# The last attention period of a fused adaLN, attention and two-stage expert kernel, re-ordered on one core

## What is computed

```python
xc  = modulated(x, cond) @ W          # scaled by cond, then demodulated
q, k, v = split(xc @ w_qkv.T); q, k = rope(q), rope(k)     # 16 heads of 8
p   = softmax(causal(q @ k.T / sqrt(8)))
x1  = x + (p @ v) @ w_out.T
s   = sigmoid([x1, cond] @ W_router.T); the two best of s + bias give the gates
x2  = (shared_experts(x1) + sum_e gelu(x1 @ r_w1[e].T) @ r_w2[e].T * gate_e) / 4
w   = softmax weights of the best 3 of 8 zones, from tanh(mean(x2) @ W1 + b1) @ W2 + b2
out = x1 + x2 + sum_z gelu(x2 @ Wa[z]) @ Wb[z] * w_z
```

## Time and profile before

| | us |
|---|---|
| median of 3 runs (lowest, highest) | 181.64 (181.29, 181.72) |
| the profiled execution | 180.98 |
| its span | 179.1 |
| PE busy | 168.9 |
| DVE busy | 138.9 |
| ACT busy | 134.3 |
| POOL busy | 93.8 |

### The profile page before, as it was taken

The page is one execution under the profiler, slowest core; times in us unless marked ns, Lnnn a source line. Parts: engine busy times, 40 slices in busy tenths (PEclk is TensorE's granted clock), DMA queues, the critical chain, the costliest instruction groups (busy, mean ns, idle before and its releaser), DMA issues.

```text
span 179.1 us, 3278 instructions
## 1 busy us (share of the span) xinstructions
PE 168.9 (94%) x943; PEld 116.8 (65%) x944; DVE 138.9 (78%) x444; ACT 134.3 (75%) x224; POOL 93.8 (52%) x117
## 2 busy tenths in 40 slices
PE   6899999899999999988999999996999989999992
PEld 2656575565666666653758767864687867788881
DVE  5588989989898899980586999699799658637551
ACT  3569177688768888889734787953879999999970
POOL 5508088985463969688532522021769931676000
PEclk9999999999999999999999999999999999999999
DMA  4824775676686567520110899960760000001001
GB/s 144 294 46 107 191 203 159 218 234 213 166 267 208 143 194 194 164 94 5 62 51 17 231 345 344 347 178 4 241 230 0 0 4 0 0 2 59 0 4 59
DMA packets 15349, 24.28 MB, mean 136 GB/s; under 512 B 2844, under 2 KB 4828, under 8 KB 15308
## 3 DMA queue, kind: packets, MB, share of 16 engines
q1 hardware_dynamic: 14532, 23.29, 42.2%
q10 hardware_dynamic: 800, 0.79, 1.7%
HBM read 18.71 MB, written 5.27 MB: 134 GB/s over the span
## 4 chain that ended last, share of the span: by engine, by line
PE 70%; DVE 11%; ACT 7%; issue 6%; POOL 4%; DVEq 0%; ACTq 0%; POOLq 0%
PE psum L1407 11%; PE psum L1540 10%; PE psum L1541 9%; PE psum L1542 9%; PE psum L1467 8%; PE psum L1443 7%; PE psum L1286 3%; PE psum L1338 2%; PE psum L1352 2%; ACT t_probs L1105 2%; DVE psum L772 2%; DVE t_raw L924 1%; PE psum L1402 1%; ACT t_q_pad L1155 1%; PE psum L1447 1%
## 5 line engine op out<-in xcount | busy, mean ns | idle before, releaser
L772 DVE CUSTOM_DVE_ANT_0 psum<-psum,t_causal 128x128 f32<-128x128 f32 (+3 forms) x128 | 58.6, 525 | 5.8 <-PE psum L1407 3.0
L1105 ACT ACTIVATE t_probs<-psum 128x1024 f32<-128x1024 f32 (+2 forms) x48 | 40.9, 883 | 8.2 <-PE psum L1443 5.2
L1407 PE MATMUL psum<-t_stacked,t_q_pad 96*128 96x256 f32 (+2 forms) x104 | 33.3, 391 | 0.5 <-DVE t_row_max L772 0.2
L1407 PEld LDWEIGHTS psum<-t_stacked,t_q_pad 96*128 96x128 f32 x104 | 18.4, 189 | 12.4 <-DVE t_row_max L772 10.2
L672 POOL TENSOR_SCALAR_AFFINE_SELECT t_probs<-t_probs 128x512 f32<-128x512 f32 x32 | 20.5, 651 | 9.0 <-ACT t_probs L1105 9.0
L944 DVE SCALAR_TENSOR_TENSOR t_q_pad<-psum,t_zw_all,t_q_pad 128x512 fp32r<-128x512 f32 x24 | 17.8, 748 | 9.3 <-ACT t_q_pad L1153 9.2
L1139 ACT ACTIVATE psum<-psum 128x512 f32<-128x512 f32 x40 | 23.4, 586 | 0.9 <-PE psum L1542 0.3
L703 POOL TENSOR_TENSOR t_q_pad<-t_raw,t_q_pad 128x512 fp32r<-128x512 f32 x8 | 10.8, 1357 | 21.0 <-ACT t_q_pad L1155 21.0
L1467 PE MATMUL psum<-t_probs,t_v_all 128*32 128x512 f32 (+3 forms) x256 | 20.6, 439 | 0.0
L772 DVE DVE_READ_ACCUMULATOR2_ANT t_row_max<- 128x1 f32 x128 | 18.0, 141 | 0.0
L1153 ACT ACTIVATE t_q_pad<-psum,t_zw_all 128x512 fp32r<-128x512 f32 x24 | 16.5, 688 | 1.2 <-PE psum L1542 0.6
(11 more groups left out here) (233 smaller groups left out, 369.6 us busy)
## 6 DMA issues: line engine op xcount, KB each, us to landing
t_stacked<-scratch SPq DMA_DIRECT2D x16, 256.0 KB, 5.7
t_probs<-in_L_ffn_Wa SPq DMA_DIRECT2D x2, 1024.0 KB, 11.5
scratch<-t_o_sb SPq DMA_DIRECT2D x7, 256.0 KB, 2.1
t_raw<-in_experts SPq DMA_DIRECT2D x7, 256.0 KB, 3.6
t_stacked<-scratch SPq DMA_DIRECT2D x9, 192.0 KB, 3.7
t_q_pad<-scratch SPq DMA_DIRECT2D x28, 48.0 KB
scratch<-t_dn_hi SPq DMA_DIRECT2D x2, 512.0 KB, 3.4
t_q_two<-scratch SPq DMA_DIRECT2D x5, 192.0 KB, 2.6
```

The lines of the kernel that those rows point to most:

```text
L772: last = V.tensor_tensor_reduce(scores, scores, causal[:, S - width:S], 1.0, 3 * BIG, ALU.add, ALU.max, row_max[s][:, qb, j:j + 1])
L1105: A.activation(o, scores, ACT.Exp, scale=float(1.0 / np.sqrt(np.float32(HD)))).then_inc(exp_done, 1)
L1407: last = T.matmul(bank[:, o:o + width], q_pad[s][0:TOP, j, qb * P:(qb + 1) * P], stacked[0:TOP, n, 0:width], start=True, stop=True)
```

## The change

Seven edits, all in the order of work; nothing of the arithmetic changes.

1. The laying of group 7's maxima goes to a ring bank (7) and not to a half of the exp slots. POOL places them after the first mask of period 6, not before the second. The copy of the laid rows goes from ACT to DVE, behind `residual(0)`.
2. `normalise(0)` on DVE goes from behind unit (7, 10) to behind (7, 7), `project_out(0)` on PE from period 7 to period 6.
3. In period 6 PE has scores 3, the projection, the laying, scores 4 and 5, and V product 0 last.
4. Period 7 is written out on PE: V products 1 to 3 of group 6 stand between the scores of group 7, the router behind them, then scores 2 to 5, `up(0)`, and all V products of group 7.
5. The router's logits lie in bank 7, their exp is taken behind exp 1 of group 7.
6. Splits and loads of the expert weights come half a period earlier.
7. `take_outputs(6)` on DVE goes behind the high and low parts of x1. `invert(1)` goes from ahead of the unit loop to i = 1, `normalise 1` from i = 3 to 4.

```diff
-RING_ORDER += [("out", 0), ("route", 0)]
+RING_ORDER += [("out", 0), ("lay", GROUPS - 1)]
+LAST = GROUPS - 1
 AT = {
-    "normalise 1": [3],
+    "invert 1": [1],
+    "normalise 1": [4],
...
-INV_AT = [(6, 8), (7, 10)]
-SPLITS = {(3, 0): 0, (3, 2): 1, (4, 0): 2, (4, 2): 3, (5, 0): 4, (5, 2): 5, (6, 0): 6}
-EXPERT_LOADS = [(), (0, 1), (2, 3), (4, 5), (6,), (), (), ()]
+INV_AT = [(6, 8), (7, 7)]
+SPLITS = {(2, 2): 0, (3, 0): 1, (3, 2): 2, (4, 0): 3, (4, 2): 4, (5, 0): 5, (5, 2): 6}
+EXPERT_LOADS = [(), (0, 1, 2), (3, 4), (5, 6), (), (), (), ()]
...
         def qm_bank(n):
-            return ST[:, slot_of("exp", n - 1, STU - 1) + 1, :] if n else ring("lay", 0)
+            return ST[:, slot_of("exp", n - 1, STU - 1) + 1, :] if 0 < n < LAST else ring("lay", n)
...
-                    if c == 1 and n + 1 < GROUPS:
+                    if c == 1 and n + 1 < LAST:
                         place_max(n + 1)
                     for o in ((0,) if c < 2 else (0, 2 * P)):
...
                     last.then_inc(masked, 1)
+                    if c == 0 and n + 1 == LAST:
+                        place_max(LAST)
...
+            def copy_last_qm():
+                dve.wait_ge(qm_full, GROUPS)
+                V.tensor_copy(q_mov[LAST % BUFS][TOP:ROWS, :], qm_bank(LAST)[TOP:ROWS, :]).then_inc(qm_copied, 1)
...
-            take_outputs(GROUPS - 2)
             residual(0)
+            copy_last_qm()
             x1_high(0)
             x1_low(0)
+            take_outputs(LAST - 1)
             dve.wait_ge(w_lo, len(range(0, UP_COLS, S)) + len(range(0, DN_COLS, S)))
             gates(0, 0) ... gates(0, 3)
-            invert(1)
             for i in range(N_UNITS + 1):
                 if i < N_UNITS:
                     finish_hidden(i)
                 if i:
                     hidden_lo(i - 1)
+                for _ in due("invert 1", i):
+                    invert(1)
...
-                bank = (ring("route", 0) if b == 0 else MISC)[:, 0:KB * EXPERTS]
+                bank = (MISC if b else QM)[:, 0:KB * EXPERTS]
...
                 exp(n, 1)
+                if n == LAST:
+                    exp_of_minus_logits(0)
...
-                if n + 1 < GROUPS:
+                if n + 1 < LAST:
                     copy_qm(n + 1)
-                if n == GROUPS - 1:
-                    exp_of_minus_logits(0)
...
-                    wait_ring("route", 0)
+                    pe.wait_ge(qm_copied, GROUPS)
...
-                    pe.wait_ge(expneg, 1)
+                    pe.wait_ge(mx_reduced, len(MX_LIST))
+                    pe.wait_ge(x1_ready, 1)
...
-            for n in range(GROUPS):
+            for n in range(LAST):
...
                 scores_for_exp(n, 2)
-                if n == GROUPS - 1:
+                scores_for_exp(n, 3)
+                if n + 1 == LAST:
                     project_out(0)
-                scores_for_exp(n, 3)
+                    lay_max_under_q(LAST)
...
                 scores_for_exp(n, 4)
-                if n == GROUPS - 1:
-                    route_experts(0)
+                if n + 1 == LAST:
+                    scores_for_exp(n, 5)
                 weigh_v(n, 0, 0, S)
...
+            scores_for_exp(LAST, 0)
+            weigh_v(LAST - 1, 1, P, S)
+            scores_for_exp(LAST, 1)
+            weigh_v(LAST - 1, 2, 2 * P, S)
+            weigh_v(LAST - 1, 3, 3 * P, S)
+            route_experts(0)
+            scores_for_exp(LAST, 2)
+            scores_for_exp(LAST, 3)
+            scores_for_exp(LAST, 4)
+            scores_for_exp(LAST, 5)
             up(0)
-            weigh_v(GROUPS - 1, 1, P, S)
-            weigh_v(GROUPS - 1, 2, 2 * P, S)
-            weigh_v(GROUPS - 1, 3, 3 * P, S)
+            weigh_v(LAST, 0, 0, S)
+            weigh_v(LAST, 1, P, S)
+            weigh_v(LAST, 2, 2 * P, S)
+            weigh_v(LAST, 3, 3 * P, S)
```

More of the change, by code:

```diff
@@ L1412, in lay_max_under_q @@
                 pe.wait_ge(m_ready, n + 1)
-                if n:
+                if 0 < n < LAST:
                     wait_slot("exp", n - 1, STU - 1)
                 else:
-                    wait_ring("lay", 0)
+                    wait_ring("lay", n)
                 if n == 0:
@@ L1528, in route_experts @@
                 if b == 0:
-                    wait_ring("route", 0)
-                bank = ring("route", 0) if b == 0 else MISC
+                    pe.wait_ge(qm_copied, GROUPS)
+                bank = MISC if b else QM
                 T.matmul(bank[:, 0:KB * EXPERTS], temb[:, b, :], small[:, W_RT:W_RB], start=True, stop=True)
@@ L1659, in _ @@
                 scores_for_exp(n, 4)
-                if n == GROUPS - 1:
-                    route_experts(0)
+                if n + 1 == LAST:
+                    scores_for_exp(n, 5)
                 weigh_v(n, 0, 0, S)
-                maximum(7)
-                if n + 1 < GROUPS:
+                if n + 1 < LAST:
+                    maximum(7)
                     lay_max_under_q(n + 1)
-                maximum(8)
-                scores_for_exp(n, 5)
-                maximum(9)
-                maximum(10)
+                    maximum(8)
+                    scores_for_exp(n, 5)
+                    maximum(9)
+                    maximum(10)
+            scores_for_exp(LAST, 0)
[8 more added lines that the diff above has]
+            scores_for_exp(LAST, 5)
             up(0)
-            weigh_v(GROUPS - 1, 1, P, S)
-            weigh_v(GROUPS - 1, 2, 2 * P, S)
-            weigh_v(GROUPS - 1, 3, 3 * P, S)
+            weigh_v(LAST, 0, 0, S)
+            weigh_v(LAST, 1, P, S)
+            weigh_v(LAST, 2, 2 * P, S)
+            weigh_v(LAST, 3, 3 * P, S)
             for i in range(1, N_UNITS + LAG):
```

## The result

The changed kernel takes **184.94 us** (median of 4 runs, 183.93 to 186.01); the kernel before, run beside it, 181.68 (181.29 to 181.75). The ratio is 1.0196, 95% interval [1.016, 1.0232]. The change costs 3.3 us where the forecast said 0.7, outside its range of 180.7 to 183.0. The profiled execution took 185.37, its span 183.6, 4.5 more than before.

A forecast was written before the change was run, and what follows sets the result against it. It took the PE-led chain of waits, and when DVE's residual(1) runs, as the bound. +1.0 for the late residual(1) less 0.25 slack gave +0.75, stated as +0.7: median 182.3 us, range 180.7 to 183.0.

The forecast's parts named there:

- (2): DVE, period 6: normalise(0) moved forward collides with POOL's spreading and delays unit (7, 8) by 1.45 us.
- (4): PE, group 7 in the new order: second up starts at 93.25 against 93.56, 0.3 us gained.
- (5): invert(1) 3.1 us later; DVE waits for gate rows until 104.2; residual(1) at 108.9 against 107.89, 1.0 us later.
- (1): Splits and expert loads half a period earlier on ACT and SP: cost 0, at most 0.8 us, once.
- its sign of being wrong: An exp of period 3 that waits for ACT's split would show the splits and loads mispriced.
- the far end given: Upper delay for unit (7, 8): 2.1 us, if normalise(0) waits behind POOL's low part also, 79.17.
- the row in the middle: Delay of 1.45 us for unit (7, 8), from the DVE cast's row: 0.53 us beside POOL's masks.
- (3): Period 6: laying in a ring bank, POOL's place after the first mask; laying at 81.5 instead of 81.97, 0.5 gained.
- laying at 81.5, so 0.5 gained: PE, period 6: the laying for group 7 comes at 81.5 instead of 81.97, counted as 0.5 us gained.
- PE's gain: The 0.3 us by which PE's second up was to start earlier, 93.25 against 93.56.
- (6): Behind residual(1): small waits of DVE and ACT for PE soak up 0.25 us, taken from 0 to 0.5.

The follow-up runs named there:

- e9: Changed kernel with the sixth split moved to period 6's first place, so POOL has no low part behind the last spread; 183.45 us, ratio 1.014.
- e15: Changed kernel with two warm-up matmuls ahead of scores (7, 4) and the inverse behind unit 0 instead of unit 1; 183.54 us, ratio 1.0095.
- e5: Changed kernel with the splits and expert loads of before; 186.0 us, ratio 1.0213.
- e4: Kernel before with normalise(0) alone moved forward behind unit (7, 7); 182.26 us, ratio 1.0056.
- e6: e3 with normalise 1 at i = 3 and the splits and loads of before; 182.0 us, ratio 1.0037.
- e8: Kernel before with only invert(1) moved to i = 1 and normalise 1 to i = 4; 184.7 us, ratio 1.0142.
- e10: Kernel before with invert(1) moved behind finish_hidden(0), normalise(1) left at 3; 181.02 us, ratio 0.9984.
- e14: Changed kernel with two warm-up matmuls ahead of scores (7, 4) and nothing else; 185.13 us, ratio 1.0201.
- e1: Changed kernel with normalise(0) back behind unit (7, 10); 183.78 us, ratio 1.0129.
- e3: Changed kernel with normalise(0) back behind (7, 10), invert(1) at i = 0 and PE's projection behind the laying; 182.71 us, ratio 1.0051.
- e11: e6 with scores (6, 4) and V product (6, 0) ahead of the laying again; 182.1 us, ratio 1.0071.
- e2: Changed kernel with invert(1) alone moved up to i = 0, behind finish_hidden(0); 184.28 us, ratio 1.0179.
- e7: e3 with five warm-up matmuls in PE's wait for the maxima at 80 us; 182.49 us, ratio 1.007.
- e12: e6 with two warm-up matmuls in PE's wait at 90 us, ahead of scores (7, 4); 181.42 us, ratio 0.9999.

## Why the prediction was wrong

The forecast was +0.7 us, measured was +3.3. Four steps failed: the delay by `normalise(0)` in (2), 1.45 forecast and 2.64 measured; the stretch on PE in (4), 10.7 and 11.4; DVE's wait for the gate rows in (5), 1.8 and 3.0 to 3.3; and TensorE's clock, which stood in no term. Where the collision has the forecast's price (e9), the change costs 1.6 at full clock.

**(1) Splits and loads** at 0: its sign of being wrong, an exp that waits for ACT's split, is in the profile of e15 (ACT waits 1.97), and PE waits 0.2 to 1.2 for the padded queries in four others (e5). The forecast had the group's own loads behind them not due for a period, and 0.8 as the most that all this could cost; the stretch lost 1.1 and 1.2 in two of eight profiles.

**(2) `normalise(0)`** was the first term mis-sized. The collision was seen and the row taken as the nearest was the cast (one input in SBUF, not two) that ended after one of POOL's masks, hence 1.45. Measured: 2.64 for the unit behind it (77.60 to 80.24), beyond even the far end given, 2.1. That end was the end of POOL's low part; the operation still has to run after it, which the row in the middle had counted and the far end had not. The Trainium skill, page "SBUF — State Buffer", section "Summary: rules for kernel authors", says that the later of two such instructions "fully blocks" until the first is finished. The trace agrees with the blocking and adds what the page does not say: it can last through two POOL instructions in a row (2.72 us in the changed kernel and in e4), and the operation ends 0.55 after the last of them (in e9, with one of them to wait for, 1.48).

**(3) and (4) The laying and group 7 on PE** failed by themselves, with no help from (2). The place of the laying was right: e9 has it at 81.4. But the second `up` is 0.3 later than before there, not 0.3 earlier, and in e6, where the laying is earlier still, it is 0.8 later: the step "laying at 81.5, so 0.5 gained" took the laying as the event that counts, and the work that had covered the wait stood behind it. I also priced scores 0 and 1 of group 7 at 0.45 each; they take 0.64 and 0.68 (the row of four in the earlier trace rows, 1.42, would have said 0.7), so with V products and scores 2 and 3 the stretch from V product (6, 0) to the second `up` is 11.4 (e6 and e9) and not 10.7. With it the router is late, and the gates start 0.6 later than the forecast's 87.4 in e9 and 1.9 later in the changed kernel (89.87 less its shift).

**(5) The late inverse** was the right mechanism, with the direction of the result, and too small. The chain was timed well: DVE free at 102.4 was forecast, and e8 has it at 102.5 after its shift of 0.8. What was wrong is the landing, forecast for 104.2: in e8 the inverse runs at 98.7 (shift taken off), 0.5 later than the forecast without PE's gain, and the first finish comes 4.0 behind the issue of the gate rows, not 3.5. The row itself lands 3.8 to 4.1 after its issue in the changed kernel, e8, e9 and e10; the 3.5 was one row of one execution. DVE's wait is then 3.1 instead of the forecast's 1.8 (102.4 to 104.2), and the first routed finish 2.3 later than before instead of 0.9. Its cost at full clock is 1.3 (e8), against the +1.0 of my step, which was to hold the collision and PE's gain too.

**(6) The slack of 0.25** is hardly seen: `residual(1)` is 4.7 late and the span 4.5 longer; in e9 it is 1.7 late and the time 1.6 longer.

**What was not in the forecast at all** is the clock. It had PE's two waits for exp, 0.5 and 0.25 us, in its sum, and took each for its own length.

The account of the 3.3 us, at full clock first: late inverse 1.3 (e8, 182.67 against 181.33) and order of periods 6 and 7 about 0.3 (e6, full, 181.68 against 181.33), together the 1.6 of e9. The full runs of the changed kernel and of e14 lie 2.5 to 2.7 above before (184.22 and 184.04, against 181.68 and 181.39), so POOL's low part in the collision is about 1.0 of it, which is what is left and not a measurement of its own; the whole collision costs 0.7 in the order of before (e4, full, 182.11 against 181.39). Two or three runs stand behind some of these parts, e5 does not fit them, and the loads of (1) may hold some tenths. The rest, 0.7, is the clock's fall in half the runs, worth 1.3 to 2.2 us each time (low less full medians of e1 to e3, e5 to e9, e11 and e14).

## What to carry to other kernels

When a wait is moved ahead of independent work in an in-order queue, price what used to run in that wait, not how early the awaited thing comes (e6, where nothing ran in it, against e9). Before a two-input SBUF operation of DVE is moved, list what POOL has queued from that moment, all of it. And a hand-over has a due time: moved by less than its slack it is free (e10), beyond it the whole queue behind it waits (e8). A landing time read from one execution is no bound: the same chunk landed 4.4 us after its issue in one profile and 6.1 in another.

## What was not expected of the hardware

- A short idle time of PE can cost more than itself. In 18 of 44 runs of the five kernels with the new order of period 7, PE idle for 0.55 us at 90 us and no wait for gate rows (e2, e3, e6, e7, e11), the mean granted clock was 0.991 or less. In profiles with the fall it is 0.50 for about 3 us. Two matmuls without use in that wait took it away in e12 (0 of 12, where e6 has 5 of 12). The 1.41 us of idle time at 80 us did not have this effect (e7).
- Two of POOL's operations one behind the other kept a DVE operation of 0.69 us waiting for 2.72; with a mask as POOL's second it was 1.48 and the mask waited, 1.09 instead of 0.63. In both it ended 0.55 after the operation that it had waited for.
